# First attention of a four-stage kernel: two heads side by side in TensorE's rows, the value products in halves, transfers in place of the output transposes

## The reference, cut to what matters

```python
q = _split(lora_linear(x, Wq, bq, Bq, Aq))        # 16 heads of 16 features
k = _split(lora_linear(x, Wk, bk, Bk, Ak))
v = _split(lora_linear(x, Wv, bv, Bv, Av))
scores = jnp.einsum('bhqd,bhkd->bhqk', q, k) * SCALE
attn = jax.nn.softmax(scores, axis=-1)            # over 1024 keys, no mask
out = jnp.einsum('bhqk,bhkd->bhqd', attn, v)
out = out.transpose(0, 2, 1, 3).reshape(B, L, H * hd)
return lora_linear(out, Wo, bo, Bo, Ao)
```

## Time and profile before

| | us |
|---|---|
| median of three runs | 3302.27 (3302.18 to 3310.47) |
| the profiled execution, its own time | 3307.49 |
| its span, first to last instruction | 3305.7 |
| TensorE busy | 3098.8 (94%) |
| VectorE busy | 2139.0 (65%) |
| ScalarE busy | 1854.7 (56%) |
| POOL busy | 1111.6 (34%) |
| mean granted clock of TensorE | 0.982 of full speed |

### The profile page before, as it was taken

How to read it: one execution, slowest core, us unless ns; L and a number is a source line. 1 busy time by engine, 2 the same in 40 slices (tenths; PEclk the granted TensorE clock), 3 DMA queues, 4 the chain that set the end, 5 groups by cost and what they waited for, 6 DMA issues and landing times. The chain is left out here.

```text
span 3305.7 us, 62515 instructions
## 1 busy us (share of the span) xinstructions
PE 3098.8 (94%) x21586; PEld 2208.1 (67%) x21586; DVE 2139.0 (65%) x6393; ACT 1854.7 (56%) x4670; POOL 1111.6 (34%) x1753
## 2 busy tenths in 40 slices
PE   7999999979999999996987999999999999999998
PEld 5888888822333333333776888788877888778886
DVE  5776666658888888874755555555556555555555
ACT  4666666627767767673445555455554555445553
POOL 1111111010010010002015556575555655566554
PEclk9999999979999999997999999999999999999999
DMA  4111111042223132101324434354343443244432
GB/s 137 42 41 43 40 44 37 15 83 38 51 47 67 27 71 42 29 8 55 132 75 107 98 89 96 92 121 97 79 113 86 112 98 89 65 112 101 97 83 65
DMA packets 310379, 241.68 MB, mean 73 GB/s; under 512 B 150768, under 2 KB 256688, under 8 KB 309936
## 3 DMA queue, kind: packets, MB, share of 16 engines
q1 hardware_dynamic: 310064, 237.69, 29.2%
HBM read 100.71 MB, written 39.85 MB: 43 GB/s over the span
## 5 line engine op out<-in xcount | busy, mean ns | idle before, releaser
L1660 ACT ACTIVATE b_pp<-b_pp,b_nm 128x192 f32<-128x192 f32 (+2 forms) x1024 | 472.5, 463 | 458.5 <-DVE b_nm L1828 377.0
L903 DVE TENSOR_REDUCE a_mx<-ps 128x1 f32<-128x512 f32 x1024 | 636.5, 681 | 88.3 <-PE ps L851 88.2
L825 ACT ACTIVATE a_pt<-ps 128x512 f32<-128x512 f32 x1024 | 534.9, 601 | 245.1 <-PE ps L862 243.6
L1630 POOL TENSOR_SCALAR b_pp<-b_pp,b_rc 128x192 f32<-128x192 f32 x960 | 388.0, 430 | 441.1 <-DVE b_rc L1837 441.1
L1849 DVE COPY b_pt<-ps 128x384 f32<-128x384 f32 (+2 forms) x336 | 182.0, 555 | 388.1 <-PE ps L1749 369.7
L851 PE MATMUL ps<-a_k,a_q 96*128 96x512 bf16 x1024 | 399.3, 391 | 18.9 <-DMA a_k<-qk_parts 16.1
L862 PE MATMUL ps<-a_q,a_k 99*128 99x512 bf16 x1024 | 387.4, 382 | 8.9 <-issue 5.4
L1828 DVE CUSTOM_DVE_ANT_0 b_pp<-ps,b_mk 128x192 f32<-128x192 f32 x960 | 276.3, 353 | 130.8 <-PE ps L1728 130.8
L638 DVE SCALAR_TENSOR_TENSOR f_yac<-ps,f_cw,f_yac 128x128 f32<-128x128 f32 x992 | 276.6, 343 | 122.2 <-PE ps L447 120.7
L851 PEld LDWEIGHTS ps<-a_k,a_q 96*128 96x128 bf16 x1024 | 100.1, 98 | 292.1 <-issue 152.6
L447 PEld LDWEIGHTS ps<-w,f_sq 128*128 128x128 f32 x2048 | 264.9, 191 | 29.7 <-DVE f_yac L638 7.2
(11 more groups left out here) (254 smaller groups left out, 7104.3 us busy)
## 6 DMA issues: line engine op xcount, KB each, us to landing
b_rt<-b_qf SPq DMA_DIRECT2D x1024, 64.0 KB, 2.0
qk_parts<-f_aa SPq DMA_DIRECT2D x32, 384.0 KB, 2.6
a_q<-qk_parts SPq DMA_DIRECT2D x192, 64.0 KB, 3.0
a_k<-qk_parts SPq DMA_DIRECT2D x96, 128.0 KB, 5.2
...
```

What stands on the lines that cost most here:

```text
L825: e.activation(pt[(4 * i + j) % 8][:, :], P.ap(s), ACT.Exp).then_inc(P.free_sem(s), 1)
L903: e.tensor_reduce(mx[kh % 3][:, j * 4 + t, h:h + 1], P.ap(s), AX.X, ALU.max, negate=True).then_inc(P.free_sem(s), 1)
L1630: m = e.tensor_scalar(x, x, r[:, 2 * u + h:2 * u + h + 1], 1.0, ALU.mult, ALU.mult)
L1660: e.activation(x, x, ACT.Exp, bias=nm[n % 4][:, c:c + 1], scale=-1.0, accum_out=sm[n % 4][:, c:c + 1]).then_inc(exp_done, 1)
```

## The change

In the first half the projections are split in two fp32r parts instead of three bf16 parts: ScalarE writes the first from PSUM, VectorE the rest from PSUM in one operation, and POOL has no part in it. `qk_parts` becomes an f32 tensor of two parts.

In the first attention one head takes 48 rows (three blocks of 16) and two rows for the negated maxima, and two heads lie in one buffer, at partitions 0 and 64. A step `max` or `score` is now a pair of products, one in each half of TensorE's rows, with a bank each. The maxima have two pairs of banks, 0 and 1, 2 and 3, and one reduction for the pair; the scores rotate through banks 4 to 6; the products with the values have bank 7 alone and are made in two halves of 256 queries, the second of which comes one pair of scores later than the first. `pt` has 12 buffers. The transposed maxima are split in two parts by VectorE alone and go in by four transfers. The ones for those rows come from memsets over 32 partitions, two for each of the three buffers, and the first load waits for all of them.

After eight i ScalarE evacuates bank 7 into `ev`, and eight transfers close the heads up: values into `og`, sums (16 equal rows for a head) into `sg`, with features in the partitions. A new step `norm`, once for each half batch, takes the reciprocal of `sg` on VectorE (two operations of 128 x 512) and multiplies on POOL; `three` multiplies `og` directly with the output weights. The steps `one` and `two` are gone.

The eight transfers of an evacuation stand ahead of the load, and the next row transfers stand behind it. The diff, cut to its core:

```diff
+    def pair(self, step):
+        i = self.at[step][0]
+        return self.ps[:, i:i + 2, :]
...
+                    w.wait_ge(aa_out[m % 2], 16 * (m // 2))
+                    e.activation(aa[m % 2][:, 0, :], P.ap(s), ACT.Identity,
+                                 bias=M["bqk"][:, n, h:h + 1]).then_inc(aa_high, 1)
...
+                    n, h, m = s[2] // 2, s[2] % 2, 4 * c + s[2]
+                    w.wait_ge(aa_high, m + 1)
+                    e.scalar_tensor_tensor(out=aa[m % 2][:, 1, :], in0=P.ap(s), scalar=M["bqk"][:, n, h:h + 1],
+                                           in1=aa[m % 2][:, 0, :].bitcast(F32), op0=ALU.add,
+                                           op1=ALU.subtract).then_inc(P.free_sem(s), 1)
...
-        n = min(slot + 48, 36 + slot * 10 // 8, 64 * units)
+        n = min(slot + 24, 18 + slot * 10 // 8, 32 * units)
         while emitted < n:
             out.append(("max", emitted))
             emitted += 1
-            if emitted % 32 == 0:
-                out.append(("both", emitted // 32 - 1))
-                late.append((slot + (2 if slot else 0), ("rows", emitted // 32 - 1)))
+            if emitted % 16 == 0:
+                out.append(("both", emitted // 16 - 1))
+                late.append((slot + (1 if slot else 0), ("rows", emitted // 16 - 1)))
         return out
 
     p += ahead(0)
     while late:
         p.append(late.pop(0)[1])
-    p += [("score", 0, j) for j in range(4)]
+    p += [("score", 0, j) for j in range(2)]
...
-        for j in range(4):
-            p += ahead(4 * i + j + 1)
-            if i + 1 < 16 * units:
-                p.append(("score", i + 1, j))
-        p.append(("pv", i))
+        p += ahead(2 * i + 1)
+        if i + 1 < 16 * units:
+            p.append(("score", i + 1, 0))
+        if c:
+            p.append(("pv", i - 1, 1))
+        if (c == 2 or c >= 4) and side:
+            p.append(side.pop(0))
+        p += ahead(2 * i + 2)
+        if i + 1 < 16 * units:
+            p.append(("score", i + 1, 1))
+        p.append(("pv", i, 0))
         if c == 7:
-            p.append(("evac", i // 8))
+            p += [("pv", i, 1), ("evac", i // 8)]
             if u % 4 == 3:
+                n = 2 * (u // 4) + h
+                side += [("norm", n)] + [("three", 4 * n + t) for t in range(4)]
                 if i + 1 == 16 * units:
-                    p += side
-                    side = [("last",)]
...
-    KS, KX = 96, 99
+
+    parts = ((0, 1, 0), (0, 0, 1))
+    KS, KX = 48, 50
...
-                P.take(s, s[1] % 3)
+                P.take(s, 2 * (n_max % 2), 2 * (n_max % 2) + 1)
+                n_max += 1
             elif s[0] == "score":
-                P.take(s, 3 + (4 * s[1] + s[2]) % 3)
-            elif s[0] == "pv":
-                group = s[1] // 8
-                if s[1] % 8 == 0:
-                    P.take(("group", group), 6 + group % 2, fills=False)
+                for a in range(2):
+                    P.take((*s, a), 4 + n_score % 3)
+                    n_score += 1
+            elif s[0] == "pv" and s[1] % 8 == s[2] == 0:
+                P.take(("group", s[1] // 8), 7, fills=False)
...
+        qs = [sb(f"q{i}", [128, 2, 2, CH], FR) for i in range(3)]
+        ks = [sb(f"k{i}", [128, 2, L], FR) for i in range(3)]
         vs = [sb(f"v{i}", [128, 8, H0, 32]) for i in range(2)]
-        pt = [sb(f"pt{i}", [128, CH]) for i in range(8)]
-        mx = [sb(f"mx{i}", [128, 16, 2]) for i in range(3)]
+        pt = [sb(f"pt{i}", [128, CH]) for i in range(12)]
+        mx = [sb(f"mx{i}", [128, 2, 8, 2]) for i in range(3)]
...
+        n2 = [sb(f"n2{i}", [16, 2, 128], FR) for i in range(2)]
+        ev = [sb(f"ev{i}", [128, CH]) for i in range(2)]
+
+        og = [sb(f"og{i}", [128, 2, CH]) for i in range(2)]
+        sg = [sb(f"sg{i}", [128, 2, CH]) for i in range(2)]
...
+                    w.wait_ge(ones_set, 3)
                     if n >= 3:
-                        w.wait_ge(*P.filled(("score", 16 * (n - 3) + 15, 3)))
...
+                        w.wait_ge(*P.filled(("score", 16 * (n - 3) + 15, 1, 1)))
...
+                    for a in range(2):
+                        for r in range(3):
+                            rows = slice(64 * a + 16 * r, 64 * a + 16 * r + 16)
+                            src = [X["qk"][m, parts[m][r], g * 64:(g + 1) * 64, b * L:(b + 1) * L].rearrange(
+                                "(p a d) t -> a d p t", p=2, a=2)[a] for m in range(2)]
+                            for h in range(2):
+                                e.dma_start(qs[i][rows, h, :, :].bitcast(F32),
+                                            src[0][:, :, h * CH:(h + 1) * CH]).then_inc(q_in[i], 16)
+                            e.dma_start(ks[i][rows, :, :].bitcast(F32), src[1]).then_inc(k_in[i], 16)
...
+                    w.wait_ge(*P.emptied(s))
+                    for a in range(2):
+                        for r in range(2):
+                            dst = qs[i][64 * a + KS + r:64 * a + KS + r + 1, h, :, :]
+                            e.dma_start(dst.rearrange("a p (t q) -> a (p t) q", q=128).bitcast(F32),
+                                        n2[n % 2][8 * a:8 * a + 8, r, :].bitcast(F32)).then_inc(rows_in[i][h], 16)
+                elif k == "evac":
+
+                    z, g, h = n // 8, n // 2 % 4, n % 2
+                    z = 2 * z + h
+                    w.wait_ge(*P.emptied(("group", n)))
+                    if z >= 2:
+                        w.wait_ge(*P.filled(("three", 4 * (z - 2) + 3)))
+                    for j in range(4):
+                        r = slice(64 * (g % 2) + 16 * j, 64 * (g % 2) + 16 * j + 16)
+                        e.dma_start(og[h][r, g // 2, :], ev[n % 2][32 * j:32 * j + 16, :]).then_inc(og_in[h], 16)
+                        e.dma_start(sg[h][r, g // 2, :], ev[n % 2][32 * j + 16:32 * j + 32, :]).then_inc(og_in[h], 16)
+                elif k == "norm":
+                    if n == 0:
+                        residual(e, w, 0)
+                        residual(e, w, 1)
+                elif k == "three" and n + 2 < 8 * B:
+                    residual(e, w, n + 2)
...
-                e.memset(k6[i][KS:KX, :, :], 1.0).then_inc(ones_set, 1)
+                e.memset(ks[i][32:64, :, :].bitcast(F32), 1.0)
+                e.memset(ks[i][96:128, :, :].bitcast(F32), 1.0).then_inc(ones_set, 1)
             for s in plan:
                 k, n = s[0], s[-1]
-                if k == "rows":
...
+                if k == "norm":
+                    for c in range(2):
+                        x = og[n % 2][:, c, :]
+                        w.wait_ge(rc_ready, 2 * n + c + 1)
+                        e.tensor_tensor(x, x, sg[n % 2][:, c, :], ALU.mult).then_inc(norm_done, 1)
...
+                    if i >= 3:
+                        w.wait_ge(pv_done, pv_at[i - 3, 1])
+                    for a in range(2):
+                        w.wait_ge(*P.filled((*s, a)))
+                        e.activation(pt[(4 * i + 2 * j + a) % 12][:, :], P.ap((*s, a)),
+                                     ACT.Exp).then_inc(P.free_sem((*s, a)), 1)
                 elif k == "evac":
...
+                    w.wait_ge(pv_done, pv_at[8 * n + 7, 1])
+                    if n >= 2:
+                        z = n - 2
+                        w.wait_ge(og_in[z % 2], 128 * (z // 2 + 1))
+                    e.activation(ev[n % 2][:, :], P.ap(("group", n)),
                                  ACT.Copy).then_inc(P.free_sem(("group", n)), 1)
...
+                    u, half, j, t, h = n // 32, n // 16 % 2, n // 8 % 2, n // 2 % 4, n % 2
                     w.wait_ge(q_in[u % 3], 192 * (u // 3 + 1))
                     w.wait_ge(k_in[u % 3], 96 * (u // 3 + 1))
-                    e.matmul(P.ap(s), q6[u % 3][0:KS, half, j, t * 128:(t + 1) * 128],
-                             k6[u % 3][0:KS, j, h * CH:(h + 1) * CH], start=True, stop=True).then_inc(P.full_sem(s), 1)
+                    for a in range(2):
+                        r = slice(64 * a, 64 * a + KS)
+                        m = e.matmul(P.pair(s)[:, a, :], qs[u % 3][r, half, j, t * 128:(t + 1) * 128],
+                                     ks[u % 3][r, j, h * CH:(h + 1) * CH], start=True, stop=True)
+                    m.then_inc(P.full_sem(s), 1)
...
+                        w.wait_ge(*P.before((*s, a)))
+                    for a in range(2):
+                        r = slice(64 * a, 64 * a + KX)
+                        e.matmul(P.ap((*s, a)), ks[u % 3][r, j, c * 128:(c + 1) * 128], qs[u % 3][r, h, j, :],
+                                 start=True, stop=True).then_inc(P.full_sem((*s, a)), 1)
...
+                    x = slice(256 * half, 256 * half + 256)
                     w.wait_ge(v_in[b % 2], 16 * (b // 2 + 1))
-                    if c == 0:
+                    if c == half == 0:
                         w.wait_ge(*P.before(group))
                     for j in range(4):
-                        w.wait_ge(*P.emptied(("score", n, j)))
```

(17 more changed lines are left out.)

163 lines of the change are left out of this document (34 added, 129 removed).

## The result

The changed kernel is slower: 3413.82 us (3400.57 to 3428.59, four runs) against 3303.56 (3302.18 to 3310.47, four), a ratio of 1.033, 95% interval 1.028 to 1.038. Forecast was 3284, at most 3345. The profiled execution took 3428.59, the slowest of the four; it is 121 us over the profiled one of before (3307.49), where the medians differ by 110.

A forecast was written before the change was run, and what follows sets the result against it. The prediction took TensorE's own issue rate in the first attention as the bound. Its terms, -71 us there, +44 for the division and +9 at the start, gave -18 on 3302.27: 3284 us, range 3235 to 3345.

The forecast's parts named there:

- Slot 1.25 us: First attention: TensorE's time for one maxima pair, one score pair and half the value products, 0.34 + 0.33 + 0.58 us.
- pairs overlap: First attention: two products in separate halves of TensorE's rows run together, bounds 0.23 us a pair overlapped, 0.46 not.
- reduction 1.15: VectorE in the first attention: a maxima reduction over 2 x 512 elements takes 1.15 us in a row, at most 1.36.
- loop under the slot: Scores waiting for ScalarE's first exponential of the pair before: 1.08 us, under TensorE's 1.25, so TensorE stays the bound.
- Rivals C and D: C: dearer reductions make VectorE the bound, 3334, 14%; D: pairs don't overlap, about 3500, partial overlap 3330, 7%.
- the 71 us: First attention without division and start cost: 720 us instead of 790.8, the forecast's gain.
- Hidden, with 2 us to spare: Row transfers behind loads on SP's queue: 19 us against 21 available, so no wait for the scores.
- M waits 4.9 us, 2.5 for the clock: Maxima products behind VectorE's division: 7.4 us each with clock recovery, six norms, +44 us.
- Start +9: Start of the first attention: first load waits for six memsets, 11 us; less 1.6, with smaller changes, +9, at most +19.
- the 4 us allowed: Slower clock at the start of the first attention: 4 us more, included in the stage's 720.
- The end, nothing: Norm, product and residual after the first attention's last values: 24 us as before, so no change.
- Rival B: First attention: stalls of 0.7 and 0.45 us get hidden (-35) and the clock stays up (-15): 3234 us, 22%.

## Why the prediction was wrong, step by step

- **Slot 1.25 us, pairs overlap, reduction 1.15, loop under the slot: right in mechanism.** S to S took 1.25 to 1.33; the reduction 1.22, off by 0.07; an ordinary half without a stop 21.9 against 22.5 (which held an output tile that the 21.9 doesn't; with one, 22.8, so 0.3 to 0.4 too low). Rivals C and D didn't come. Of the 71 us 50 are shown: the kernel with split loads and later last products has the whole stage, division included, in 740.6 us, where before it took 790.8. Of the rest 13 are its cold start (17 us in halves 0 and 1, where 4 were priced).
- **"Hidden, with 2 us to spare" failed first.** It cost the most, though not all: with it mended, in the kernel with split loads, the time was still 39 us above before. The step added up issues and took the landing, 1.7, from rows of before, which there were issued 9 us or more behind the last load, mostly when the loads had landed. The half that holds the rows shown began at 830.0 and needed them at 851.6, 21.5 us later, as reckoned (21). Their issue ended at 850.25, after 20.2 us and not 17.2, and the score began 9.8 us after that, not 1.7; where no values stood ahead (805.4), it was 4.9. So TensorE waited 2.5 to 3.8 us behind a load (1.3 once) and 8.3 to 8.7 where the values stood ahead too: 49.5 us in eleven halves, and the clock behind each. The 23 ordinary halves averaged 26.0 us, where they average 22.0 with the loads late: 92 us. In the medians the late loads gave 54 us back, less than that among other things because the first norms of the pairs became dearer, and the split 16 more.
- **"M waits 4.9 us, 2.5 for the clock" was mis-sized, less than the first.** Reciprocals took 3.3, as priced at 3.5. But TensorE didn't go on for 2.5 slots, 3.3 us: at the second norm VectorE began to divide at 969.93 and TensorE stopped at 971.67, 1.7 us later; at the first, where VectorE had stood 1.71 us for the sums' transfer, 0.4 later. The wait was 5.9 to 7.3. With the loads split, the stop with its clock was 7.6 in the half shown and 8.2 in the mean of six, against 7.4. In the changed kernel itself a norm half was 35.5, and taking the division out saved 9.1 of it.
- **The clock was priced per stop, from one row of before, and capped at 2.5 us.** The price behind a stop was another each time. The kernel before never stopped TensorE for over 2 us between the first score and the end of the values; the changed one does so sixteen times for over 2 us. Behind a stop of 2 to 14 us the clock stayed at 1.2 GHz for 3 to 24 us, in each trace of the changed kernel twice for 38 to 48. Those two, 82 us in the first trace, where 17 (10.2 + 6.8) went by in the kernel without division, cost 65 x (1 - 1.37/2.21) = 25 us, with 1.37 us for a warm slot (21.9/16) and 2.21 for a cold one (half 5, 35.4/16). This is worked out, not an experiment.
- **Start +9: 5, the sum of two things, one of them luck.** The first score came 5.2 us later. The six memsets took 11.0 as I had taken, but the first half, where I had put nothing, let them begin 5.9 us earlier. The clock there cost more than the 4 us allowed: halves 0 and 1 took 58 us instead of 49, and 56 to 71 in the other kernels made from it. With the loads split they took 71, so there the start alone was 22 us over the sum.
- **The end, nothing: 7 us.** From the last exponential to the program's end 1807.8 us, before 1800.5.
- **Rival B** (3234) said the stalls would drift apart. They don't; where a plan removes them, the gain is there, at 3270.

I had looked at each wait by its slack, and the largest risk was a transfer that had to land in time: its 2 us to spare were added up with a landing time from a trace in which the loads were mostly over by then.
